# Attention stage of a two-layer kernel: denominators one pair later, turned maxima in another ring, big loads from another queue

## The reference

```python
qkv = (h @ Wqkv.T + bqkv).reshape(B, N, num_heads, hd, 3)     # 16 heads of 32
energy = jnp.einsum('bhqd,bhkd->bhqk', q, k)
att = jax.nn.softmax(energy, axis=-1) / D ** 0.5
out = jnp.einsum('bhqk,bhkd->bhqd', att, v)
out = out @ Wp.T + bp
h1 = out + hidden
return _sln(h1, ...) + h1
```

## Time and profile before

| | us |
|---|---|
| median of 3 runs | 1877.42 |
| lowest, highest | 1874.85, 1879.06 |
| the profiled execution, its own time | 1878.27 |
| its span, first to last instruction | 1876.5 |
| PE busy | 1817.7 (97%) |
| DVE busy | 1250.9 (67%) |
| ACT busy | 778.2 (41%) |
| POOL busy | 1175.8 (63%) |

### The profile page before, as it was taken

The page is one execution under the profiler, slowest core; times in us unless marked ns, Lnnn a source line. Parts: engine busy times, 40 slices in busy tenths (PEclk is TensorE's granted clock), DMA queues, the critical chain, the costliest instruction groups (busy, mean ns, idle before and its releaser), DMA issues. The chain is left out here.

```text
span 1876.5 us, 26949 instructions
## 1 busy us (share of the span) xinstructions
PE 1817.7 (97%) x9542; PEld 1217.3 (65%) x9542; DVE 1250.9 (67%) x2054; ACT 778.2 (41%) x1376; POOL 1175.8 (63%) x654
## 2 busy tenths in 40 slices
PE   8989999999999999999999999999999999999995
PEld 4678888888887788888555455545554555554584
DVE  4655655655655444546777777777777777777399
ACT  3213123122222222221466666666666666666200
POOL 2665465465464112111589888888898888888455
PEclk9999999999999999999999999999999999999998
DMA  7410110110103555474787778877887878765893
GB/s 268 118 34 23 57 34 22 56 34 22 56 1 129 192 202 190 165 237 141 180 176 177 168 180 188 180 166 183 185 184 169 185 177 183 177 148 139 266 400 144
DMA packets 131014, 278.47 MB, mean 148 GB/s; under 512 B 23846, under 2 KB 41382, under 8 KB 122840
## 3 DMA queue, kind: packets, MB, share of 16 engines
q1 hardware_dynamic: 98772, 191.71, 33.8%
q0 software_dynamic: 9264, 66.11, 17.3%
q10 hardware_dynamic: 22872, 19.28, 3.2%
HBM read 134.42 MB, written 75.80 MB: 112 GB/s over the span
## 5 line engine op out<-in xcount | busy, mean ns | idle before, releaser
L1612 DVE TENSOR_REDUCE at_mrow<-banks 128x1 f32<-128x512 f32 x976 | 593.5, 679 | 166.3 <-PE banks L1458 166.2
L1708 POOL TENSOR_TENSOR at_sums<-at_probs 128x2048 f32<-128x2048 f32 x127 | 597.6, 4706 | 90.9 <-DMA at_sums<-at_sums 81.1
L1592 ACT ACTIVATE at_probs<-banks 128x512 f32<-128x512 f32 x1024 | 519.2, 623 | 183.8 <-PE banks L1476 178.7
L1458 PE MATMUL banks<-early_ks,early_qs 96*128 96x512 f32 x976 | 406.8, 417 | 9.7 <-DVE at_mrow L1612 5.7
L1476 PE MATMUL banks<-early_qs,early_ks 98*128 98x512 f32 x1024 | 408.7, 418 | 2.2 <-ACT at_probs L1592 1.8
L1458 PEld LDWEIGHTS banks<-early_ks,early_qs 96*128 96x128 f32 x976 | 184.7, 189 | 142.1 <-DVE at_mrow L1612 88.2
L1476 PEld LDWEIGHTS banks<-early_qs,early_ks 98*128 98x128 f32 x1024 | 193.6, 190 | 107.0 <-ACT at_probs L1592 82.7
L1488 PE MATMUL banks<-at_probs,at_v 128*32 128x512 f32 x2048 | 249.8, 605 | 1.4 <-DMA at_v<-v_scratch 1.4
L71 PE MATMUL banks<-l_nt,l_weights 128*128 128x512 f32 x768 | 179.3, 394 | 5.4 <-DVEq L1198 4.3
L71 PE MATMUL banks<-l_ht,l_weights 128*128 128x512 f32 x768 | 177.5, 390 | 1.9 <-issue 1.9
L71 PE MATMUL banks<-l_weights,l_hf 128*128 128x512 f32 x768 | 177.5, 390 | 0.0
(11 more groups left out here) (148 smaller groups left out, 2072.6 us busy)
## 6 DMA issues: line engine op xcount, KB each, us to landing
at_sums<-at_sums POOLq DMA_DIRECT2D x63, 1024.0 KB, 8.1
qk_scratch<-qk_out SPq DMA_DIRECT2D x64, 512.0 KB, 2.8
early_ks<-qk_scratch SPq DMA_DIRECT2D x48, 512.0 KB, 5.1
early_qs<-qk_scratch SPq DMA_DIRECT2D x96, 256.0 KB, 5.6
attn_scratch<-at_out SPq DMA_DIRECT2D x32, 512.0 KB, 7.4
o_a<-attn_scratch SPq DMA_DIRECT2D x32, 512.0 KB, 12.6
chunk_in<-x SPq DMA_DIRECT2D x8, 1024.0 KB, 5.4
v_scratch<-qk_v ACTq DMA_DIRECT2D x32, 256.0 KB, 2.4
```

Of the source, the lines that this page charges most:

```text
L1458: pe.matmul(em[n % 3][:], qs[0:96, slot, half, j, c * P:(c + 1) * P], ks[0:96, slot, j, keys * CH:(keys + 1) * CH], start=True, stop=True) ...
L1592: nc.scalar.activation(probs[:, i % 4, j, :], et[n % 3][:], ACT.Exp).then_inc(exp_done, 1)
L1612: nc.vector.tensor_reduce(mrow[:, half, keys, u:u + 1], em[n % 3][:], AX.X, ALU.max).then_inc(max_done, 1)
L1708: nc.gpsimd.tensor_tensor(into, probs[:, a], probs[:, a + 1], ALU.add).then_inc(pair_ready, 1)
```

## The change

- Denominators come behind even pairs, with `LAG` = 4, one pair later. A quad's first sum has three buffers (two of `sums` and a free half of the projection weights' place), the second sum two (the third of `sums` and the other half). The landing of accumulates is counted on two semaphores.
- A turn no longer uses the denominators' bank. It takes a place of its own in the ring of the three maxima banks: `place` counts it between the maxima products, PE waits until that bank's last reduction is done, and VectorE counts the negation as a reduction.
- All loads of stacks, values, projection weights and the first projection chunks are issued by ScalarE, behind its last exponential of pairs 1, 3, 5 and 7. They no longer wait for accumulates. SP keeps the small transfers and the stores, in a new order.
- ScalarE's and VectorE's work on denominators and POOL's work on the halves follow one pair later. The projection's weights are loaded and split in group 15.

```diff
-        LAG = 3
+        LAG = 4
+        LAST_QUADS = QUADS * (G - 1)
+        def first_sum(q):
+            if q < LAST_QUADS:
+                return (sums[:, 0], sums[:, 1], sh.wp_first)[q % 3]
+            return sums[:, q % 2]
+        def second_sum(q):
+            return sh.wp_raw if q < LAST_QUADS and q % 2 else sums[:, 2]
+        def first_free(q):
+            return q - 3 if q < LAST_QUADS + 2 else q - 2
+        def second_free(q):
+            return q - 2 if q <= LAST_QUADS else q - 1
+        def landed(q):
+            return quad_ready[q % 2], 16 * (q // 2 + 1)
...
+        def place(n):
+            return n + (n - FIRST_MAXIMA + 8) // (2 * UNITS)
+        def turn_place(g, half):
+            k = halves(g, half) - 2
+            return min(FIRST_MAXIMA + 24 + 2 * UNITS * k, 2 * QH * UNITS * G) + k
...
 # sync, group(): load_part and load_projection leave SP
-                fetch(0)
+                place_neg(g, slot, 1)
                 if not first:
                     spread_den(g - 1, 1)
+                    widen_rden(g - 1, 1)
                     store(g - 1, 0)
-                place_neg(g, slot, 1)
-                if not first:
-                    widen_rden(g - 1, 1)
-                fetch(1)
-                fetch(2)
+                if with_next:
+                    place_neg(g + 1, (slot + 1) % RING, 0)
                 spread_den(g, 0)
+                widen_rden(g, 0)
                 if not first:
                     store(g - 1, 1)
-                if with_next:
-                    place_neg(g + 1, (slot + 1) % RING, 0)
-                widen_rden(g, 0)
-                fetch(3)
 # tensor
             def turn_max(g, half):
-                pe.wait_ge(max_done, 2 * UNITS * halves(g, half))
-                if halves(g, half) > 2:
-                    pe.wait_ge(den_taken, halves(g, half) - 2)
+                pe.wait_ge(max_done, turn_place(g, half) - 2)
+                pe.wait_ge(max_done, place(2 * UNITS * halves(g, half) - 1) + 1)
+                bank = em[turn_place(g, half) % 3]
...
-                    if p % 2 == 1:
+                    if p % 2 == 0:
                         den_before(g, p)
             groups(pe, group)
+            den(G - 1, QUADS - 2)
 # scalar
+            def load_part(g, slot, part):
+                if part == 0:
+                    if g > 2:
+                        act.wait_ge(av_done, STEPS * (g - 2))
+                    load_stack_keys(act, sh, ks, g, slot, (0,))
+                    load_stack_queries(act, sh, qs, g, slot, 0, (0,))
+                if part == 1:
+                    load_stack_keys(act, sh, ks, g, slot, (1,))
+                    load_stack_queries(act, sh, qs, g, slot, 0, (1, 2))
+                if part == 2:
+                    load_stack_keys(act, sh, ks, g, slot, (2,))
+                    load_stack_queries(act, sh, qs, g, slot, 1, (0,))
+                if part == 3:
+                    load_stack_queries(act, sh, qs, g, slot, 1, (1, 2))
+                    act.dma_start(v[:, slot], sh.v_d[g]).then_inc(stack_loaded[slot], 16)
+            def load_projection(g, part):
...
+                if part == 1:
+                    act.wait_ge(*landed(LAST_QUADS - 1))
+                    act.dma_start(wp_raw[:], wp_t.rearrange("(k p) n -> p k n", p=P)).then_inc(wp_loaded, 16)
+                if part == 2:
+                    load_attended(act, sh, 0, range(2, KT))
+                if part == 3:
+                    load_style(act, sh, 0)
+                    load_residual(act, sh, 0)
+                    load_attended(act, sh, 1)
+                    load_residual(act, sh, 1)
+                    load_style(act, sh, 1)
...
-                    if g == 1 and i % KC in (3, 5):
-                        split_wp(2 * (i // KC) + (i % KC - 3) // 2)
+                    if i % 4 == 3:
+                        if not with_next:
+                            load_projection(g, i // 4)
+                        elif load:
+                            load_part(g + 2, (slot + 2) % RING, i // 4)
+                    if not with_next and i >= STEPS - KT:
+                        if i == STEPS - KT:
+                            act.wait_ge(den_done, LAST_QUADS)
+                        split_wp(i - STEPS + KT)
                     if i % KC == KC - 1:
                         take_av(g, i // KC)
-                    if i == 3 and not first:
+                    if i == 5 and not first:
                         take_den(g - 1, 1)
-                    if i == KC + 3:
+                    if i == KC + 5:
                         take_den(g, 0)
 # vector: negate_max works in the turn's bank, then
+                dve.wait_ge(negt_taken, halves(g, half))
+                dve.sem_inc(max_done, 1)
...
-                    if p == 2 and not first:
+                    if p == 3 and not first:
                         invert(g - 1, 1)
-                    if p == SPAN + 2:
+                    if p == SPAN + 3:
                         invert(g, 0)
 # gpsimd: multiply, round_off, remain one pair later; sums into first_sum(quad), second_sum(quad)
-                    if second and quad >= 1:
-                        pool.wait_ge(quad_ready, 16 * quad)
-                    if not second and quad >= 2:
-                        pool.wait_ge(den_done, quad - 1)
+                    if second and second_free(quad) >= 0:
+                        pool.wait_ge(*landed(second_free(quad)))
+                    if not second and first_free(quad) >= 0:
+                        pool.wait_ge(den_done, first_free(quad) + 1)
```

More of the change, by code:

```diff
@@ L1287, in attention_stage @@
         av_done, av_taken = sem("at_av_done"), sem("at_av_taken")
-        pair_ready, quad_ready = sem("at_pair_ready"), sem("at_quad_ready")
+        pair_ready, quad_ready = sem("at_pair_ready"), [sem(f"at_quad_ready{i}") for i in range(2)]
         den_done, den_taken = sem("at_den_done"), sem("at_den_taken")
@@ L1336, in _ @@
         def _(sp):
[L1337 to L1372, removed]
             def load_v(g, slot):
@@ L1453, in max_unit @@
             def max_unit(g, slot, half, u, keys):
-                n, j, c = number(g, half, u, keys), u // TT, u % TT
+                n, j, c = place(number(g, half, u, keys)), u // TT, u % TT
                 if n >= 3:
@@ L1503, in den @@
                     for j in range(HG):
-                        last = pe.matmul(den_ps[HD * j:HD * (j + 1), cols], ones_col[:], sums[:, q % 2, j, cols],
+                        last = pe.matmul(den_ps[HD * j:HD * (j + 1), cols], ones_col[:], first_sum(q)[:, j, cols],
                                          start=n == 0 and part == 0, stop=n == QUADS // QH - 1 and part == PARTS - 1)
@@ L1570, in take_av @@
                 nc.scalar.activation(av_sb[:, half], av_ps[:], ACT.Copy, scale=SOFTMAX_SCALE).then_inc(av_taken, 1)
+            def load_part(g, slot, part):
[14 more added lines that the diff above has]
+            def load_projection(g, part):
+                if part == 0:
+                    act.wait_ge(av_done, STEPS * g)
+                    for half in range(QH):
+                        act.wait_ge(out_free[half], 16 * (KT + 1))
+                    load_attended(act, sh, 0, range(2))
+                if part == 1:
[9 more added lines that the diff above has]
+                    load_style(act, sh, 1)
             def split_wp(k):
@@ L1611, in take_max @@
                 dve.wait_ge(e_done, n + 1)
-                nc.vector.tensor_reduce(mrow[:, half, keys, u:u + 1], em[n % 3][:], AX.X, ALU.max).then_inc(max_done, 1)
+                nc.vector.tensor_reduce(mrow[:, half, keys, u:u + 1], em[place(n) % 3][:], AX.X, ALU.max).then_inc(max_done, 1)
             def negate_max(g, half):
-                joined = den_ps[0:UNITS, 2 * P:3 * P]
+                bank = em[turn_place(g, half) % 3]
+                joined = bank[0:UNITS, 2 * P:3 * P]
                 dve.wait_ge(mrow_turned, halves(g, half))
-                nc.vector.tensor_reduce(joined, den_ps[0:UNITS, 0:2 * P].rearrange("u (k c) -> u c k", c=P), AX.X, ALU.max).then_inc(maxima_joined, 1)
+                nc.vector.tensor_reduce(joined, bank[0:UNITS, 0:2 * P].rearrange("u (k c) -> u c k", c=P), AX.X, ALU.max).then_inc(maxima_joined, 1)
                 dve.wait_ge(maxima_joined, halves(g, half))
@@ L1687, in group @@
             def group(g, slot, nth=None, first=False, load=True, with_next=True):
-                for pair in range(PAIRS if with_next else PAIRS - 1):
+                for pair in range(PAIRS):
                     if not first:
                         for half in range(QH):
-                            if pair == SPAN * half:
+                            if pair == SPAN * half + 1:
                                 multiply(g - 1, half)
-                            if pair == SPAN * half + 1:
+                            if pair == SPAN * half + 2:
                                 round_off(g - 1, half)
```

(14 more changed lines are left out.)

21 lines of the change are left out of this document (7 added, 14 removed).

## The result

The changed kernel takes 1906.94 us (median of 4 runs, 1902.65 to 1910.56) against 1876.79 for the kernel before on the same chip: ratio 1.0156, interval 1.0134 to 1.0179. It is slower by 30 us where 1871 was forecast. Its profiled run has a span of 1900.9 us.

The account below looks back on a forecast made before the run. PE was taken as the bound, with 21.2 us of waits in groups 1 to 14. 1878.3 - 21.2 + 10.1 + 0.7 + 1.5 - 1.4 + 3.3 = 1871.3: forecast 1871 us, range 1860 to 1888.

Parts of the forecast that it names:

- the last sentence on SP's order: Reciprocals' way to memory and back, then POOL's multiply: moved one pair with POOL's operations, as far ahead as now, no cost.
- Waits that go, -21.2: PE's waits in attention, groups 1 to 14, about 0.76 us per half: they go, 21.2 us saved.
- Turn, +10.1: PE waits for the sixth reduction before each turn: 0.36 us in each of 28 turns, 10.1 us added.
- Residue of the small transfers, 1.5: VectorE's reciprocal waiting for gathered denominators: flight up to 4.7 us is free, 1.5 us left over 28 halves.
- Rival 1: Small transfers stay slow: gathered denominators late at VectorE, PE loses 36 us in place of 1.5, 1906 us; chance 0.14.
- ScalarE's issues free: Load issues behind ScalarE's last exponential of odd pairs, 1.3 us for three, fit before the next exponential: no cost.
- Start, -1.4: Projection weights and three stack loads no longer run beside the first v: 1.4 us of PE's wait go.
- Tail, +3.3: Group 15's weight split and the reciprocal behind it delay the output stage: at least 1.5, up to 5, taken as 3.3.

Follow-up runs that it names:

- e5: Changed kernel with POOL's product written over the reciprocals and POOL's three operations one pair later; 1872.30 us, ratio 0.9978 to the kernel before.
- e6: Changed kernel with a sixteenth of the bytes in each stack load of groups 3 to 15; 1873.22 us, ratio 1.0011 to the kernel before.
- e7: Changed kernel with a sixteenth of the columns in each accumulate; 1873.10 us, ratio 1.0002 to the kernel before.
- e3: Changed kernel with VectorE's reciprocal of the last group's first half ahead of the split weights; 1898.62 us, ratio 1.0113 to the kernel before.
- e10: e8 with the turn's two transposes between the value products of the pair's two steps; 1871.74 us, ratio 0.9996 to the kernel before.
- e13: e8 with POOL's rounding made five times in place of once; 1882.22 us, ratio 1.0033 to the kernel before.
- e8: e5 with the edit of e3 added; 1870.34 us, ratio 0.9997 to the kernel before; again 1871.91 us, 0.9986.

## Why the prediction was wrong

- **The step that failed** is the last sentence on SP's order: the queue after the reciprocal "has moved one pair with POOL's three operations, so it stays as far ahead as now". The table above shows both halves of it wrong. Before, the last broadcast lands at 29.9 us and the multiply starts at 30.5, so "as far ahead" was 0.6 us. With the change and POOL on time (e5) it lands at 38.4: the reciprocal moved by 5.8, one pair, the four broadcasts take 3.9 us longer from first issue to last landing, and 1.2 are gained between the two. The multiply, where nothing holds POOL and it stays one pair later only (e6, e7), is due at 35.3, 4.8 later than before: a pair for POOL is one sum of 4.7 us, and before, POOL was late anyway, by the 78.3 us of waits for accumulates that the change took away. So the multiply is 3.1 us early each half, and POOL can spare 2.5; with the broadcast as fast as before (e7) the reciprocals land at 34.4, 0.9 ahead of it. The rest closes the loop: POOL's accumulates go out 11.2 us after the odd pair's start in the changed kernel and 9.5 in e5 (medians), the gathering flies longer under them, the reciprocal starts at 27.6 instead of 25.1, VectorE's maxima and with them PE are late, and POOL waits again. This loop is read from the medians; what the runs show is that it ends when POOL's operations move (e5) or the broadcast is fast (e6, e7). Price 28.3 us, which I had at nothing. I asked of POOL only that a sum be ready in time, and never added up its half group against PE's 26.1 us.
- **Waits that go, -21.2**: right. e5 has 1 us of them left, and 731.7 / 28 = 26.1 us a half group, forecast 26.2.
- **Turn, +10.1**: a wait as described, but 0.24 us each and not 0.36: 6.7 us in 28. The transposes start 0.06 us after the sixth reduction's end, where I had taken 0.18 from the eighth product.
- **Residue of the small transfers, 1.5**: small, as forecast, by itself. With POOL on time VectorE's wait at the reciprocal is 0.0, with 4.1 us (25.1 - 21.0) from the issue of the gathering to the reciprocal against the 4.7 allowed. The 33.9 us in the changed kernel came through POOL.
- **Rival 1** gave 1906, nearly the time measured, but that is in part luck. Its path exists (VectorE stands 33.9 us for the gathered denominators, and some 12 us at PE's fronts come in by the maxima), but it is not the origin: with the same loads on ScalarE's queue and POOL on time (e5) that wait is 0.0. What was late first was the broadcast, at POOL. The rule it cites from the Trainium skill (DMA: Bandwidth & Descriptors, "Issuing engines are not separate DMA queues") is borne out in that loads on ScalarE's queue slow SP's small transfers, the write by themselves (5.2 us in e7, 1.4 in e6) and the broadcast beside an accumulate (5.8 and 2.0).
- **ScalarE's issues free**: right in groups 1 to 14. 42 key loads took 0.32 us at the median and 84 query loads 0.55 (longest 1.79), and e5's stretch leaves no room for a loss there.
- **Start, -1.4**: -1.0 measured.
- **Tail, +3.3**: 11.1. The reciprocal behind the split's subtractions was seen and taken at 3.3 where the whole +5 fell due (e3 gets 5.2 of its trace back). Not seen was what stands behind it: the ten transfers (5 MB) behind the last exponentials, whose landing ends the stage as soon as the order is mended, and ended it before the change.

## What to carry to other kernels

Before a wait is removed, add up every engine's work per period, the slow helper's too: an engine that "only waits for a DMA" may be using that wait as the delay that keeps its next operand in time. "Moved one pair later" is not one length: on each queue it is the time of what that queue does in a pair. When a transfer is given another queue, ask what else is in flight at that moment, for each hop of a chain of small transfers can pay for it: here the write paid for the loads, the broadcast for loads and accumulate together.

## What the hardware showed that I had not expected

- A 64 KB broadcast transfer lands after 2.0 us with the loads thinned (e6), 2.1 with the accumulates thinned (e7), and 5.4 to 5.8 with both at full size and at the same time (medians). The 8 KB write ahead of it lands after 1.4 us with the loads thinned (e6) and 5.2 with the accumulates thinned (e7).
- The turn's two transposes cost 0.23 us ahead of the value products where nothing is waited for (before), 0.47 with the wait for a bank (changed), and 0.46 between the value products without that wait (e10). The Trainium skill (TensorEngine Tiling (Array Packing), "Key Properties") says that a change of the tiling mode drains the engine; e10's 0.46 is compatible with that, but no run separates the drain from the transposes.
- Five roundings in a row on POOL average 0.67 us, a single one among other work 0.89 (e13, e8).
